# A layer of latent attention and a ternary linear branch: the order of weight loads and head 0's first products in the preparation stage

## The reference, cut to what matters

```python
xn = layernorm(x)                                   # 2048 tokens x 512
q = (xn @ wq.T).reshape(B, S, 16, 192)              # per head 128 "nope" + 64 rotary
kv = xn @ wkv_a.T                                   # 128 latent + 64 rotary key
kv_cache = rmsnorm(kv[..., :128], kv_norm_w)
q_lat = einsum('bshd,hdc->bshc', q_nope, wkv_b_h[:, :128])
scores = (q_lat . kv_cache + rope(q_pe) . rope(k_pe)) * SCALE, causal
out = softmax(scores) . kv_cache, then wkv_b_h[:, 128:], then wo
ffn = xn @ w_ternary.T + bias                       # w_ternary: weight rounded to -1, 0, 1 times a scale
result = x + out + ffn
```

## Time and profile before

| what | us |
|---|---|
| runs | 1764.94, 1771.49, 1775.77; median 1771.49 |
| the profiled execution | 1764.38 |
| its span, first to last instruction | 1762.6 |
| preparation within the span | 0 to 114.9 |
| from there to the fourth matmul of the first score | 114.9 to 127.4 |

### The profile page before, as it was taken

How to read it: one execution, slowest core, us unless ns; L and a number is a source line. 1 busy time by engine, 2 the same in 40 slices (tenths; PEclk the granted TensorE clock), 3 DMA queues, 4 the chain that set the end, 5 groups by cost and what they waited for, 6 DMA issues and landing times. The chain is left out here.

```text
span 1762.6 us, 27068 instructions
## 1 busy us (share of the span) xinstructions
PE 1662.0 (94%) x9030; PEld 1396.0 (79%) x9030; DVE 1180.8 (67%) x2755; ACT 820.1 (47%) x1295; POOL 963.4 (55%) x595
## 2 busy tenths in 40 slices
PE   6778999899999999999999999999999999999996
PEld 5567777677777777788888888888888888888885
DVE  6546777666776766677677777677766677676763
ACT  4334444434444453444445444455454444545452
POOL 4554444435555554555556565565656465656554
PEclk9899999999999999999999999999999999999998
DMA  7666887747666666475555555657656556555553
GB/s 275 253 221 205 273 272 231 246 125 198 177 165 167 168 179 193 129 208 153 158 138 154 164 151 162 195 153 188 158 141 165 129 152 160 145 149 135 147 130 103
DMA packets 117375, 309.08 MB, mean 175 GB/s; under 512 B 28786, under 2 KB 29299, under 8 KB 115956
## 3 DMA queue, kind: packets, MB, share of 16 engines
q1 hardware_dynamic: 89008, 227.04, 44.8%
q10 hardware_dynamic: 28228, 80.31, 16.4%
HBM read 113.25 MB, written 34.60 MB: 84 GB/s over the span
## 5 line engine op out<-in xcount | busy, mean ns | idle before, releaser
L1394 POOL TENSOR_TENSOR pT<-pT,pT_h 128x1024 fp32r<-128x1024 f32 x320 | 689.2, 2182 | 423.5 <-ACT pT_h L1283 421.6
L1141 DVE TENSOR_SCALAR_CACHE_REDUCE probs<-p_score 128x512 f32<-128x512 f32 (+3 forms) x640 | 380.9, 601 | 337.7 <-PE p_score L1065 217.3
L1262 ACT ACTIVATE probs<-probs,neg_max 128x128 f32<-128x128 f32 (+15 forms) x256 | 307.5, 1201 | 409.2 <-DVE neg_max L1147 334.8
L1283 ACT ACTIVATE pT_h<-pT 128x1024 fp32r<-128x1024 f32 x320 | 291.3, 964 | 232.7 <-PE p_out L1085 177.3
L1163 DVE STREAM_TRANSPOSE turned<-probs 128x1024 f32<-128x1024 f32 (+7 forms) x384 | 341.6, 915 | 40.7 <-ACT probs L1262 36.1
L1085 PE MATMUL p_out<-pT_h,V_h 128*128 128x256 f32 (+3 forms) x1024 | 299.7, 293 | 12.9 <-POOL pT L1394 12.9
L1085 PE MATMUL p_out<-pT,V_h 128*128 128x256 f32 (+3 forms) x1024 | 302.6, 295 | 0.0
L1085 PE MATMUL p_out<-pT_h,V_l 128*128 128x256 f32 (+3 forms) x1024 | 302.1, 295 | 0.0
L1065 PE MATMUL p_score<-Kp,qp_h 128*128 128x512 f32 (+3 forms) x640 | 236.4, 369 | 14.2 <-POOL qp_l L1386 14.0
L1065 PE MATMUL p_score<-Kn_h,q_h 128*128 128x512 f32 (+3 forms) x640 | 242.7, 379 | 2.0 <-DVE q_l L1186 1.7
L1065 PE MATMUL p_score<-Kn_l,q_h 128*128 128x512 f32 (+3 forms) x640 | 234.0, 366 | 0.0
(11 more groups left out here) (123 smaller groups left out, 2095.5 us busy)
## 6 DMA issues: line engine op xcount, KB each, us to landing
pT<-turned SPq DMA_DIRECT2D x384, 128.0 KB, 3.4
Wq<-wq_scr ACTq DMA_DIRECT2D x63, 512.0 KB, 4.3
Wv<-wv_scr SPq DMA_DIRECT2D x63, 512.0 KB, 4.2
pT<-turned SPq DMA_DIRECT2D x192, 112.0 KB, 3.9
pT<-turned SPq DMA_DIRECT2D x192, 96.0 KB, 2.5
pT<-turned ACTq DMA_DIRECT2D x128, 128.0 KB, 3.9
Wp<-wp_scr SPq DMA_DIRECT2D x31, 512.0 KB, 4.9
pT<-turned SPq DMA_DIRECT2D x192, 80.0 KB, 2.8
```

Of the source, the lines that this page charges most:

```text
L1141: dve.tensor_scalar(probs[row % ROW_RING][:, b * CW:b * CW + width], p_score[n % SCORE_RING][:, 0:width], SCALE, LOWEST, ALU.mult, ALU.max ...
L1262: act.activation(probs[row % ROW_RING][:, 0:width], probs[row % ROW_RING][:, 0:width], ACT.Exp, bias=neg_max[p][:, i:i + 1], scale=1.0, ac ...
L1283: act.activation(high.rearrange("p r t i q -> p r t (i q)"), low.bitcast(F32).rearrange("p r t i q -> p r t (i q)"), ACT.Copy).then_inc(p_ ...
L1394: pool.tensor_tensor(low.rearrange("p r t i q -> p r t (i q)"), low.bitcast(F32).rearrange("p r t i q -> p r t (i q)"), high.bitcast(F32). ...
```

## The change

- Heads 0 to 3 are combined in reverse (3, 2, 1, 0) in one buffer each, without staging; their steps are 1, 2, 5, 6, 9, 10, 13, 14. The first raw loads follow that order, and the third goes behind the tables.
- Pairs are split in steps 1, 3, 5, 7, 9, 11, 12, 13. SP issues the load of the pair of step n+1 at the head of its step n, ahead of the load of an x chunk.
- For chunks 2 and 3 the statistics move a step forward, `norm` too, and `shift` moves from the head of DVE's step 7 (11) to the end of its step 6 (10).
- Head 0's rotary and latent products, its rotation and its splits move from the head of the attention into the preparation's steps 16 and 17; `load_q(1)` stays at the head of ACT's attention list, the clearing of `turned` at the head of POOL's.
- `xhat` has 2 buffers for 3, `xb` 3 for 4.

```diff
-WEIGHT_STEPS = {1: 0, 2: 1, 3: 2, 4: 3, 12: 4, 13: 5, 14: 6, 15: 7}
+WEIGHT_STEPS = {1: 0, 2: 1, 5: 2, 6: 3, 9: 4, 10: 5, 13: 6, 14: 7}
+PAIR_STEPS = {1: 0, 3: 1, 5: 2, 7: 3, 9: 4, 11: 5, 12: 6, 13: 7}
+def early_head(w):
+    return EARLY - 1 - w // 2
+def raw_loads(g):
+    return (2 if g == 0 else 1) if g < EARLY else g // ROW_RING + 1
...
# SP
-            load_raw(sp, t, keep, stored, 0)
+            load_raw(sp, t, keep, stored, 3)
...
-            load_raw(sp, t, keep, stored, 1)
             load_x(1)
             load_pair(0)
             load_pair(1)
             load_raw(sp, t, keep, stored, 2)
...
+            load_raw(sp, t, keep, stored, 1)
             for n in range(PREP_STEPS):
+                if n + 1 in PAIR_STEPS and PAIR_STEPS[n + 1] >= 2:
+                    k = PAIR_STEPS[n + 1]
+                    sp.wait_ge(s_wp_h, k - 1)
+                    sp.wait_ge(s_wp_l, k - 1)
+                    load_pair(k)
                 if n % QB == 2 and n // QB + 2 < NCH:
...
                     load_x(cc + 2)
-                if n % 2 == 0 and 4 <= n and n // 2 < PAIRS:
...
-                    load_pair(k)
...
-                        load_raw(sp, t, keep, stored, w // 2 + ROW_RING)
+                        load_raw(sp, t, keep, stored, (0, 5, 4, 6)[w // 2])
                     store_head(w)
-                if n % 2 and n // 2 < PAIRS:
-                    store_pair(n // 2)
+                if n in PAIR_STEPS:
+                    store_pair(PAIR_STEPS[n])
...
-            sp.wait_ge(s_wq_out[1], 16 * (EARLY - 1))
-            sp.wait_ge(s_wv_out[1], 16 * (EARLY - 1))
# POOL
+            def add_rotary():
+                pool.wait_ge(rot_read, 1)
+                pool.tensor_tensor(rotated[:, :], rotated[:, :], rot_sin[:, :], ALU.add).then_inc(rot_added, 1)
+            def low_rotary():
+                pool.wait_ge(qp_high, 1)
+                pool.wait_ge(s_vl, BLOCKS)
...
-                if n % QB == 2 and n // QB + 1 < NCH:
+                if n % QB == (1 if n >= QB else 2) and n // QB + 1 < NCH:
                     norm(n // QB + 1)
...
+                if n == BLOCKS:
+                    add_rotary()
+                if n == BLOCKS + 1:
+                    low_rotary()
# ACT
+                if n in PAIR_STEPS:
+                    high_pair(PAIR_STEPS[n])
+                if n == BLOCKS + 1:
+                    high_query()
+                    high_rotary()
# DVE
-                if n % QB == 3 and n // QB + 1 < NCH:
-                    shift_of_x(n // QB + 1)
+                if n == 3:
+                    shift_of_x(1)
...
+                if n == BLOCKS:
+                    rotate(0)
+                    rotate(1)
-                if 0 <= n - 2 < BLOCKS:
+                if 0 <= n - 2 < BLOCKS and n != BLOCKS:
                     linear(n - 2)
-                if n % QB in (1, 2) and n // QB + 1 < NCH:
+                first = 0 if n >= QB else 1
+                if n % QB in (first, first + 1) and n // QB + 1 < NCH:
...
                     latent_row(n - 1)
+                if n == BLOCKS:
+                    for op in (2, 3, 4):
+                        rotate(op)
+                    linear(n - 2)
+                if n == BLOCKS + 1:
+                    split_query()
                 if n in WEIGHT_STEPS:
                     low_weights(WEIGHT_STEPS[n])
+                if n >= QB and n % QB == 2 and n // QB + 1 < NCH:
+                    shift_of_x(n // QB + 1)
# PE
+            def project(out, w, done):
+                for it in range(IT):
+                    for k, (a, h) in enumerate(((0, 0), (0, 1), (1, 0))):
+                        mm = pe.matmul(out, w[:, a, it, :], keep["xT"][:, h, it, :], start=(it == 0 and k == 0),
+                                       stop=(it == IT - 1 and k == 2))
+                mm.then_inc(done, 1)
...
+                if n == BLOCKS:
+                    pe.wait_ge(s_wp_l, PAIRS)
+                    project(p_rot, Wp[1], rot_projected)
                 if 0 <= n - 2 < BLOCKS:
                     linear(n - 2)
+                if n == BLOCKS:
+                    pe.wait_ge(s_w_l, 2 * EARLY)
+                    project(p_lat, Wq, lat_projected)
...
# attention: PE, DVE, ACT, POOL
-            project_rotary(0)
-            for it in range(IT):
-                project_latent(0, it)
...
-            for op in range(5):
-                rotate(0, op)
-            split_query(0)
...
-            high_query(0)
+            act.wait_ge(stored["wq"], 16 * EARLY)
...
             load_q(1)
-            high_rotary(0)
...
-            add_rotary(0)
-            low_rotary(0)
             pool.wait_ge(qp_ready, 2)
```

More of the change, by code:

```diff
@@ L288, in build_prepare @@
         x_in = [sb(f"x_in{i}", [P, QB, D]) for i in range(2)]
-        xhat = [sb(f"xhat{i}", [P, D]) for i in range(3)]
-        xb = [sb(f"xb{i}", [P, D]) for i in range(4)]
+        xhat = [sb(f"xhat{i}", [P, D]) for i in range(2)]
+        xb = [sb(f"xb{i}", [P, D]) for i in range(3)]
         stats = sb("stats", [P, QB, 6])
@@ L317, in build_prepare @@
         pQ = pW[:, :].rearrange("p (a c) -> p a c", a=IT)
+        p_rot, p_lat = (pX[i][:, :, :].rearrange("p a c -> p (a c)") for i in range(2))
         s_const = sem("s_const")
@@ L366, in build_prepare @@
             stored[k] for k in ("raw", "xT", "acc", "wq", "wv", "wp"))
+        rot_projected, rot_read, rot_added, lat_projected, q_high, q_split, qp_high, qp_ready = (
+            keep["query"][k] for k in QUERY_SEMAPHORES)
         block = ctx.enter_context(nc.Block())
@@ L510, in normalise @@
                     act.wait_ge(s_shift, cc + 1)
-                need(act, s_xT, m - 2)
-                act.activation(xhat[m % 3][:, :], x_in[cc % 2][:, b, :], ACT.Identity, bias=shift[cc % 2][:, b:b + 1],
+                need(act, s_xT, m - 1)
+                act.activation(xhat[m % 2][:, :], x_in[cc % 2][:, b, :], ACT.Identity, bias=shift[cc % 2][:, b:b + 1],
                                scale=rstd[cc % 2][:, b:b + 1]).then_inc(s_xhat, 1)
@@ L547, in high_weights, with high_query, high_rotary @@
             def high_weights(w):
-                g = w // 2
                 act.wait_ge(s_w, w + 1)
                 if w % 2 == 0:
-                    need(act, s_wq_out[1], 16 * (g - 1))
-                    act.activation(Wq[min(g, 1)][:, 0, :, :], pQ, ACT.Copy).then_inc(s_w_h, 1)
-                else:
-                    need(act, s_wv_out[1], 16 * (g - 1))
-                    act.activation(Wv[min(g, 1)][:, 0, :], pW[:, :], ACT.Copy).then_inc(s_w_h, 1)
+                    need(act, s_wq_out, 16 * (w // 2))
+                    act.activation(Wq[:, 0, :, :], pQ, ACT.Copy).then_inc(s_w_h, 1)
+                else:
+                    need(act, s_wv_out, 16 * (w // 2))
+                    act.activation(Wv[:, 0, :], pW[:, :], ACT.Copy).then_inc(s_w_h, 1)
+            def high_query():
+                act.wait_ge(lat_projected, 1)
+                act.activation(q_h[:, :], p_lat, ACT.Copy).then_inc(q_high, 1)
+            def high_rotary():
+                act.wait_ge(rot_added, 1)
+                for half in (slice(0, ROPE), slice(ROPE, P)):
+                    last = act.activation(qp_h[half, :], rotated[0:ROPE, :], ACT.Copy)
+                last.then_inc(qp_high, 1)
             act.dma_start(w_ffn, t["ffnT"].rearrange("p a i -> p (a i)")).then_inc(s_ffn_in, 16)
@@ L583, in _ @@
                     high_weights(WEIGHT_STEPS[n])
-                if n % 2 and n // 2 < PAIRS:
-                    high_pair(n // 2)
+                if n in PAIR_STEPS:
+                    high_pair(PAIR_STEPS[n])
+                if n == BLOCKS + 1:
+                    high_query()
+                    high_rotary()
         @block.vector
@@ L1368, in _ @@
         def _(pool):
-            issued = {"low": 0, "rotary": 0}
+            issued = {"low": 0, "rotary": 2}
             def add_rotary(g):
@@ L1444, in build @@
         }
-        stored = {}
-        for k in ("xT", "acc", "wq", "wv", "wp"):
+        for k in ("q_h", "q_l", "qp_h", "qp_l"):
+            keep[k] = [sb(f"{k}0", [P, CW], F32R)]
+        keep["query"] = {k: ctx.enter_context(nc.semaphore(k)) for k in QUERY_SEMAPHORES}
+        stored = {k: ctx.enter_context(nc.semaphore(f"{k}_stored")) for k in ("wq", "wv")}
+        for k in ("xT", "acc", "wp"):
             stored[k] = [ctx.enter_context(nc.semaphore(f"{k}_stored{i}")) for i in range(2)]
```

88 lines of the change are left out of this document (46 added, 42 removed).

## The result

The changed kernel took 1752.65 us (median of 4 runs, 1750.59 to 1753.08) where the kernel before, beside it, took 1771.13 (4 runs): the ratio is 0.9906, with an interval from 0.9881 to 0.9931, just under 1% faster. Six further runs beside eleven of the kernel before gave 1755.45 against 1769.33, a ratio of 0.9923 (0.9908 to 0.9939). The first medians stand 18.5 us apart, those of the further runs 13.9, the two profiled executions 13.8: 1764.38 before, 1750.59 after (span 1748.8). The forecast was 1757.7, from a sum of 13.8 us.

A forecast was written before the change was run, and what follows sets the result against it. PE, busy 94% of the span, was taken as the bound, so gains come only where it waits, in preparation and opening. 9.0 us to the last tile, 15.2 with drain and opening, less 1.4: 13.8 off the median, 1757.7; range 1745 to 1767.

The forecast's parts named there:

- First part: Preparation up to pair 2's landing: still behind the `xT` store, one 512 KB store less ahead, landing at 49.85 for 51.1.
- Second part: Preparation from pair 2 to pair 4: `shift` 2.0 us sooner, pair 3's wait gone, pair 4 at 71.0; gain so far 5.2.
- R+21.2: Pair 4's landing, counted from its queue: 4.9 MB at 0.37 MB a us is 13.2 us, plus 2 of start.
- R: The time at which pair 2 lands in the preparation, forecast at 49.85 us.
- Third part: Preparation from pair 4 to the last tile: pair 5 no wait, pair 7 at 90.7, last tile at 97.15, gain 9.0 us.
- P4: The time at which pair 4 lands in the preparation, forecast at 71.0 us.
- Fourth part: Drain and opening: barrier at 111.65, POOL's clearing from 112.25, 15.2 us sooner; the late `load_q(1)` costs 1.4.
- T: The time of the last tile's latent product in the preparation, forecast at 97.15 us for 106.17 before.
- The signs: `wp_raw` waits in steps 5, 9, 13, not 7; `shift` 6 us after pair 2; barrier 110 to 113; `load_q(1)` releasing `p_lat`.
- Rival 1: Preparation: pairs no longer late at all, 13 us more gained, 1744.7 us; chance 0.17.
- Rival 2: Opening: 1.2 GHz clock through slot 0 and the full `load_q` wait cut the gain to 8.6, 1762.9 us; chance 0.18.
- Rival 3: Preparation: DVE stalls 7.8 us for x in each of two chunks, 15.6 in all, 1773.3 us; chance 0.05.

The follow-up runs named there:

- experiment 5: Changed kernel with ACT issuing the load of head 1's query weights in the drain, not at the attention's opening; 1751.61 us.
- experiment 1: Changed kernel with head 0's products, rotation and splits moved back to the attention's opening; 1758.7 us.
- experiment 2: Changed kernel with SP's pair loads issued two steps ahead in its list, before the `xT` store between; 1744.1 us.
- experiment 3: Changed kernel with the pair loads issued a step ahead by ACT on its own queue, SP's order otherwise the same; 1745.14 us.
- experiment 4: Changed kernel with statistics, `norm` and `shift` of chunks 2 and 3 back in their old places; 1761.08 us.
- experiment 6: Experiment 5, and DVE's first turned row waits only for the first of the two cleared buffers; 1746.54 us.
- experiment 7: Changed kernel with the edits of experiments 2, 5 and 6 together; 1738.22 us, ratio 0.9828 to the kernel before.

## Why the prediction was right, and where it was not

**The sum.** Forecast 9.0 to the last tile, and 4.8 from there (6.2 in the drain and the opening, less 1.4). Measured to the last tile: 106.17 - 99.53 = 6.6. From there to the fourth load of `Wq`: 55.5 us before (161.68 - 106.17), 50.8 after, 4.7. Together 11.4, and the 2.4 of the rest brought it to 13.8. That the total is the forecast to a tenth is chance, and of the 6.6 the earlier start made 1.2. The time itself came 5 us under the 1757.7, since I took the 13.8 off a median 7.1 above its profile, and the changed kernel's median is 2.1 above its own. That the time lay inside the range is not chance: the late pairs, `shift` and the drain are where the working had them.

**First part, right.** Pair 2 was forecast at 49.85 and came at 48.79, but chunk 1's normalising had begun 1.17 us sooner (32.05 against 33.22): at an equal start it is 49.96. I don't credit the start to the change: it lies between 31.91 and 33.16 in the experiments, which have the same first steps. The load did stand behind the `xT` store, as the working said: issued at 37.82, it landed 10.9 later, the store 11.0 after 37.15. That a load can't pass the store is the working's own inference; here all three pairs behind a store landed 0.5 to 0.6 us after it.

**Second part: `shift` right, the term "R+21.2" too small.** Pair 3 came at R+8.5, with 0.46 us of wait left where I had none. `shift` came at R+6.1 (forecast R+6.1), and the op lay beside POOL's add: 0.78 us from 54.09, ending with the add that began at 53.58. The Trainium skill, "SBUF — State Buffer", section on the two separate sides, says that a DVE operation with two inputs in SBUF and a GpSimd operation that reads SBUF share one pair of ports as an exclusive lock, the later one blocked until the other ends. The 0.78, and the 1.14 of the earlier trace rows, against 0.16 with POOL idle, agree. Pair 4 was forecast at R+21.15, with R+22.6 as the late end; it came at R+23.4. (The low end of the gain there, 3.6, should read 3.7: 76.17 - 72.45.) The step that failed is "4.9 MB at 0.37 is 13.2 us, plus 2 of start": from the issue of the x load (54.94, R+6.15) to the landing it was 17.2 us, for 15.2. I had the order of the queue right, but not what had to pass. From 54.94 to 72.17 the DMA view counts 6.17 MB, at 358 GB/s; my 4.9, in units of 1024 KB, are 5.1 in that count. Of the 1.0 besides, I estimate half as what was left of the store of `acc` (issued 51.16, landed after 5.5 us) and of pair 3 (51.69, 5.6 us): of the 1.8 MB issued from 50.80 on, 1.3 had passed by 54.94. The other half is then the head's store issued at 67.94, before the pair had landed. The rate was lower too: my 0.37 is 0.39 in that count, and 0.358 was measured.

**Third part: three terms too small.** Pair 5 was to wait nothing; ACT waited 0.90 us for it. Pair 6 was to come "about when ACT wants it"; ACT waited 2.64 us. Its load was issued at 78.42, behind a raw load (75.94) and a head's store (77.59) that I had not counted for it, and took 8.0 us. Pair 7 came at P4+21.0, for P4+19.7. From pair 7 to the last tile it was 6.34 us, for 6.45. Together with the 2.2 at pair 4 and the early start, the working is 9.0 - 2.2 - 1.3 + 0.1 + 1.1 = 6.7, for 6.6 measured.

**Fourth part, right in the drain, short on `load_q`.** The clearing starts at T+14.54, where I had T+15.1. The load of `Wq` landed in 4.9 us, at my late end; PE wanted it at 115.65, 1.6 us after the clearing's start, where I had 2.4, and waited 3.52 for it. From the clearing to the fourth load the stretch is 36.2 us, for 34.3 before: the change pays 2.0, not 1.4, and with the load moved forward (experiment 5) 3.0 come back, beyond my bound of 2.6. Of the 4.7 from the last tile on, experiment 1 gives only 3.0 to the moved products; 1.8 it leaves in place, and the working, which put all of the gain down to the move, has no term for them. That its 4.8 met the 4.7 is thus in part luck.

**The signs.** ACT waits in steps 5, 9 and 13, as foreseen, but also in 12 and a little in 7 and 11. PE's `p_lat` is released by `Wq`. POOL ends its part of the preparation at 113.76, outside 110 to 113, as T is late (99.53 for 97.15). The smaller rings, costed at nothing, show no cost: in the lists of waits from 14 to 112 us ACT's normalising waits for no transpose and POOL's add for no ternary sum.

**The rivals.** Rival 1 (pairs no longer late) did not happen, since the changed list keeps the pairs behind the stores, but its price was close: experiments 2 and 3 take the pairs from behind the stores in two ways, and take 1744.1 and 1745.1 us for the 1744.7. Rival 2 (a low clock in the opening) has its low stretch, but before had one as long. Two slices of 2 us from each, after and then before:

```profile
116.00:118.00 2.00, 0.00 (x0) 0.00 (x0) 0.27 (x3) 0.60 (x2) 2.00 (x2) 0.50 0.88 348
118.00:120.00 2.00, 0.83 (x2) 0.73 (x3) 0.00 (x0) 0.00 (x0) 2.00 (x1) 0.50 0.20 78
```

```profile
126.00:128.00 2.00, 0.60 (x4) 0.60 (x4) 0.00 (x0) 0.00 (x0) 1.86 (x3) 0.50 0.00 0
128.00:130.00 2.00, 2.00 (x10) 1.81 (x10) 0.89 (x5) 0.49 (x2) 2.00 (x1) 0.50 0.00 0
```

A granted clock of 0.50 is the lower level, 1.2 GHz. From the slices around these it holds about 6.8 us in either kernel, and about 3.4 in experiment 5, where PE does not wait for `Wq`. Each time PE had been mostly idle before: busy 0.7 of the 3 us from 121 to 124 before, 0.4 from 111 to 114 after, 0.5 from 112 to 115 in experiment 5. What differs is mostly idle time: PE works at this level for 3.9 us before (127.40 to 131.3), 3.3 after (119.17 to 122.45) and 3.4 in experiment 5 (116.6 to 120.0). So the change did not pay with the clock here, and what experiment 5 gives back is the wait and not the clock. Rival 3 (DVE waits for x) fell: DVE waits for no x load but the first, and that of chunk 3 landed in 5.5 us.

**What stays open.** How the rest divides. Of the 11.4 at the mark the earlier start made 1.2, the earlier `shift` 3.4 (experiment 4, at the last tile) and the moved products 3.0 (experiment 1). What remains, 2.1 up to the last tile and 1.8 behind it, goes by subtraction to the new order of heads, pairs and weights, which no run tried alone.

Also open is why attention, the same in all these kernels, takes from 2.7 us less to 3.5 us more from one profile to the next (the gain at the last load of `Wq` less that at the fourth: 2.7 in experiment 6, -3.5 in experiments 4 and 7). It is gained or lost at a few places, at 330 to 360, 420 to 450 and 680 to 740 us, at or soon after the change from one chunk of queries to the next; there lie the stretches of low clock, at other places in each run (330 to 340 us at a mean of 0.83 before, 0.70 after). So one profile of the whole reads a change in the preparation to some 3 us only. Which of the shift in time and the clock is the cause was not tried.

## What to carry to other kernels

A load that is "issued earlier" came earlier here only where it also moved ahead of the big transfers in its own queue, or to another queue: list what is issued ahead of it, in bytes, before counting a gain, and then try it ahead of the store or on the other queue (both worth some 9 us in the preparation). When a stage's head is pulled forward, look for the loads that its old idle time had hidden: the load of `Wq` was free for as long as the opening was slow. Measure an edit at a mark just behind the stage that it touches; the whole time adds a few us to it that come up later.

## What was not expected of the hardware

The spans of eleven executions of the kernel before, on one chip, go with their mean granted clock: 1763.6 us at 0.985, 1766.9 at 0.982, 1770.5 at 0.980. That alone is about as wide as half of this change's gain. And the DMA engines, at a busy share of 0.88 from chunk 1 to the last tile, still had room: with the pair loads moved up in SP's list, and nothing else changed, they went to 0.98 (experiment 2).
